# Routing in two phases: smaller pieces over more expert tiles, other steps for the first phase, and slots from one table

## The chip, the cores and the metric

The kernel runs on one core of a Trainium2 chip (trn2). The metric is the device time of one execution in microseconds (us), as the median of several runs. PE is TensorE (matmuls), DVE is VectorE, ACT is ScalarE, POOL is GpSimd, SP is SyncE, which only issues DMAs.

## The reference, cut to what matters

64 images are cut into 36 patches each, normalised and projected to 256 features; with one class token and 32 text tokens that is 69 tokens per image, 4416 tokens in all. Then one attention layer per image (16 heads of 16) and one mixture of experts with a residual each:

```python
h = concat([tokenizer(x), txt], axis=1)              # (64, 69, 256)
h = h + attention(layernorm(h))                      # per image
xn = layernorm(h).reshape(4416, 256)
logits = xn @ router                                 # (4416, 8)
top, idx = top_k(logits, 2); gate = softmax(top)
# each token goes to its 2 experts, sorted by expert:
y = (silu(x_sort @ w13[e][:, :512]) * (x_sort @ w13[e][:, 512:])) @ w2[e]
h = h + scatter_add(y * gate)
```

## The kernel before, in words

**Two stages with a seam.** The first stage is a pipeline by hand over steps `t`, one image per step (`step(t)` on each engine). Tables such as `PJ`, `QT`, `LG`, `ZM`, `BT` say in which step a tile of 128 tokens (35 of them) has its q, k projection, its logits, or its patch projection. In step t, PE multiplies the scores of image t, DVE takes their maximum (`nm_src`, L1090), PE multiplies the scores again transposed for image t-2 (L1622, L1626) once that maximum is there, and ACT takes their exponential. A step with a projection (in `PJ`; here 46, 48, 49, 51, 53, 55, 57, 59, 61) has six matmuls of 512 columns more on PE and two large operations more on DVE (`rot`, L1136, and `qk`, L1142). Every engine works through its list in order and waits on semaphores.

From `MERGE` (step 66) on, the second stage runs: 76 expert tiles `u` of 128 token slots, in `merged(...)`. For each, POOL gathers the rows of its tokens from HBM by the indices in `token_of` (L396), PE turns them (`turn_rows`, L560), ACT and DVE split them into two halves of 16 bits (`fx_hi` L455, `fx_lo` L484), PE multiplies gate and up (`up`, 12 matmuls of 512 columns, L520), ACT takes silu (L447), DVE multiplies (L477) and splits (L491), a DMA transposes, PE multiplies down (`down`), DVE weighs the result (L500) with the token's gate (L507, L512) and POOL adds it into `out` by an indirect DMA (L419). PE's `up(u+1)` needs `fx_lo` of tile u+1, which DVE makes right behind L477 of tile u. What is left of the first stage (`drain`: the last attention steps, logits of the last token tiles, up to `LAST_STEP`) lies between these pieces, as does `route(u)`, which comes last in each u on DVE.

**The routing** says which token goes to which slot of which tile. It is done in two phases: token tiles 0 to 19 (`AHEAD`) while attention runs, so that 33 tiles that are surely full can start at step 66; token tiles 20 to 34 during expert tiles, so that the other 43 tiles are known before tile 33. The pieces, all on DVE if nothing else is said: `choose` and `choose_second` (best and second best expert per token, L934 to L952), `open_gates` (exponential of the difference, on ACT) and `gates`, `count` (one-hot tables in 16 bits), `add_places` (on PE: running numbers of the tokens per expert, by matmuls with a triangle of ones, L1458 to L1469), `rank` (picks each token's number, splits it into lane and tile number), `bases_...` and `homes_...` (first tile of each expert, tile of each token), `mark_lanes` (14 tables of 640 columns: which lane, L1037), `mark_tiles` (which tile, L1042), `number` (on POOL: times the token's number, L750), `place` (on PE, L1479), `tokens_...`, `experts_of`, `behind`, and `weigh` (on POOL: gates per expert, stored to HBM by SP). Constants like `REV ... HOMES`, `LANES`, `IN_TILES`, `NUMBERED` give the step t of each piece of the first phase, the `U_...` the tile u of the second. In DVE's step the pieces stand at the end, in the order of `step(t)`; only the patch projection's `z` (L1240) comes behind them.

In phase 1 before, `choose` is at step 47, `choose_second` 49, `gates` 51, `count` 53, `rank` 54, `bases_ahead` 55, `homes_ahead` 56, the lanes at 57 to 60 (two each), the tile tables at 59 (3), 60 (3), 61 (2), the tokens at 62. In phase 2 `choose` is at u = 6, `choose_second` and `count` at 7, `add_places` on PE and `open_gates` on ACT at 8, `rank` and `gates` 9, `bases_later` 10, `homes_later` 11 with two lanes, two lanes each at 12 and 13, tile tables 13 to 19, `place` on PE 15 to 21, `tokens_later` 22, `experts_of` 23, `behind` 24.

## Time and profile before

| what | value |
|---|---|
| three runs | 777.3, 778.82, 774.69 us (median 777.3) |
| the profiled execution's own time | 773.16 us |
| its span, first to last instruction | 771.4 us |
| busy: PE, DVE, ACT, POOL | 687.5, 559.9, 403.0, 449.9 us |
| TensorE's clock, mean of the span | 0.954 of full |

Busy time is the sum of an engine's instruction times. A window's row gives, for a stretch of the span in us, its length and each engine's busy time with the number of instructions in brackets, then the granted clock of TensorE (1.00 is 2.4 GHz, 0.50 is 1.2 GHz) and the DMA share. A timeline row gives start, duration, engine, line, operation, output and inputs with their shapes, how many were merged, and in square brackets how long the engine stood idle before it and what released it.

### The profile page before, as it was taken

What the parts mean: (1) busy time and instruction counts of PE and PEld (TensorE: products, weight loads), DVE (VectorE), ACT (ScalarE), POOL (GpSimd) and SP (SyncE); (2) the same over time, 40 slices, a digit from 0 to 9 for tenths busy, and PEclk for the clock granted to TensorE, in tenths of its full rate; (3) what the DMA queues carried; (4) which work ended last, traced back from release to release, by engine and by line L of the source; (5) the groups of instructions that cost most, each with busy time, mean ns of one, the idle gap of its engine ahead of it and who ended that gap; (6) DMA issues with size and microseconds to landing.
All of it is one profiled execution on the core that took longest, in us unless ns stands there. A gap on an engine that the chain in (4) does not pass through costs nothing. (4 is left out here: it accounts for less than half of the span.)

```text
span 771.4 us, 27556 instructions
## 1 busy us (share of the span) xinstructions
PE 687.5 (89%) x9656; PEld 477.0 (62%) x9656; DVE 559.9 (73%) x1204; ACT 403.0 (52%) x884; POOL 449.9 (58%) x632
## 2 busy tenths in 40 slices
PE   6855998999999999987978898799999999999993
PEld 4633676767667777665656565466566666666662
DVE  6876888888887888889994567966755655655652
ACT  1233567677788787777655444333344444443440
POOL 7572255556566666546544375587566666665653
PEclk9987899999999999999885999999999999999998
DMA  8677566455555465545432485677677777777863
GB/s 289 225 211 250 151 208 219 139 151 170 177 155 171 136 180 151 157 128 148 112 110 61 100 132 103 95 125 118 112 131 128 127 134 129 127 134 133 123 127 60
DMA packets 145434, 112.53 MB, mean 146 GB/s; under 512 B 93544, under 2 KB 126072, under 8 KB 145239
## 3 DMA queue, kind: packets, MB, share of 16 engines
q1 hardware_dynamic: 129927, 86.75, 42.9%
q0 software_dynamic: 15376, 24.01, 18.1%
q8 instruction: 85, 1.39, 0.8%
q14 instruction: 46, 0.38, 0.2%
HBM read 58.95 MB, written 24.90 MB: 109 GB/s over the span
## 5 line engine op out<-in xcount | busy, mean ns | idle before, releaser
L419 POOL DMA_INDIRECT out<-qk,token_of x76 | 123.1, 1620 | 99.1 <-DVE small L507 75.4
L520 PE MATMUL quad<-w_hi,fx_hi 128*128 x304 | 116.1, 382 | 12.1 <-issue 9.9
L477 DVE SCALAR_TENSOR_TENSOR probs<-quad,up_scale,vb 128x512 f32<-128x512 f32 x76 | 57.0, 751 | 88.4 <-PE quad L520 86.1
L520 PE MATMUL quad<-w_lo,fx_hi 128*128 x304 | 115.9, 381 | 0.0
L520 PE MATMUL quad<-w_hi,fx_lo 128*128 x304 | 115.7, 381 | 0.0
L520 PE MATMUL bank<-w_hi,v 128*128 x608 | 111.9, 273 | 2.5 <-DMA v<-kO 2.5
L447 ACT ACTIVATE vb<-quad,unscale 128x512 f32<-128x512 f32 x76 | 52.2, 687 | 105.1 <-PE quad L520 105.1
L1090 DVE TENSOR_REDUCE nm_src<-quad 69x16 f32<-69x1104 f32 x64 | 82.8, 1294 | 24.5 <-PE quad L1558 24.2
L1341 ACT ACTIVATE probs<-quad 69x1104 f32<-69x1104 f32 x64 | 69.7, 1088 | 57.1 <-PE quad L1626 57.1
L396 POOL DMA_INDIRECT wc<-xn_rows,token_of x73 | 74.8, 1025 | 24.0 <-issue 20.2
L520 PE MATMUL bank<-w_lo,v 128*128 x304 | 82.9, 273 | 0.0
L729 POOL TENSOR_TENSOR rs<-ve,eps_pow 128x1 f32<-128x1 f32 (+1 forms) x106 | 63.0, 594 | 8.8
L728 POOL TENSOR_SCALAR ve<-mv 128x1 f32<-128x1 f32 (+1 forms) x106 | 28.0, 265 | 64.5 <-DVE mv L1153 33.9
L520 PEld LDWEIGHTS bank<-w_hi,v 128*128 128x128 f16 x608 | 59.5, 98 | 9.0 <-issue 2.9
L764 POOL TENSOR_TENSOR h<-hb,att 128x256 f32<-128x256 f32 (+1 forms) x35 | 35.1, 1004 | 51.1 <-issue 29.8
L455 ACT ACTIVATE fx_hi<-bank 128x256 f16<-128x256 f32 x76 | 29.2, 384 | 64.2 <-PE bank L560 64.2
L1622 PE MATMUL quad<-qT,kE 32*69 32x69 f32 x1024 | 46.3, 252 | 16.5 <-DVE nm_src L1090 16.2
L772 POOL TENSOR_TENSOR qk<-rot 128x256 f32<-128x256 f32 (+1 forms) x35 | 33.4, 956 | 46.0 <-DVE rot L1136 46.0
L520 PEld LDWEIGHTS quad<-w_hi,fx_hi 128*128 128x128 f16 x304 | 29.9, 98 | 46.5 <-issue 16.1
L1622 PEld LDWEIGHTS quad<-qT,kE 32*69 32x69 f32 x1024 | 29.5, 144 | 40.4 <-DVE nm_src L1090 30.0
L1626 PE MATMUL quad<-nm,sel 32*69 32x69 bf16 x1024 | 51.6, 197 | 0.0
L520 PEld LDWEIGHTS quad<-w_hi,fx_lo 128*128 128x128 f16 x304 | 29.9, 98 | 33.0 <-issue 0.8
(282 smaller groups left out, 1770.4 us busy)
## 6 DMA issues: line engine op xcount, KB each, us to landing
w_lo<-in_experts_w SPq DMA_DIRECT2D x24, 512.0 KB, 6.1
w_raw<-in_experts_w SPq DMA_DIRECT2D x48, 256.0 KB, 4.5
xt<-in_patches SPq DMA_DIRECT2D x18, 384.0 KB, 5.6
h<-h_rows SPq DMA_DIRECT2D x34, 128.0 KB, 5.4
hb<-h_rows SPq DMA_DIRECT2D x34, 128.0 KB, 4.8
out<-h SPq DMA_DIRECT2D x34, 128.0 KB, 4.3
xn_rows<-xn SPq DMA_DIRECT2D x34, 128.0 KB, 4.8
vb<-v SPq DMA_DIRECT2D x30, 138.0 KB
```

The source lines that it names most:

```text
L396: nc.gpsimd.indirect_dma_start(xg[n % DEPTH], None, reach(xn_rows, n), bass.IndirectOffsetOnAxis(token_of[:, n:n + 1], 0)).then_inc(gather ...
L419: nc.gpsimd.indirect_dma_start(reach(out, n), bass.IndirectOffsetOnAxis(token_of[:, n:n + 1], 0), y[q], None, compute_op=ALU.add).then_inc ...
L447: nc.scalar.activation(silu[q], quad[:, 2 * q, :], ACT.Silu, scale=unscale[:, 1:2]).then_inc(d["silu_ready"], 1)
L477: nc.vector.scalar_tensor_tensor(out=hid[q], in0=quad[:, 2 * q + 1, :], scalar=up_scale[:, :], in1=silu[q], op0=ALU.mult, op1=ALU.mult).th ...
L520: last = nc.tensor.matmul(dst, x[:, k, :], w[:, bass.ds(col + k * (2 * width if width == HIDDEN else width), width)], start=(k == 0 and m ...
L729: nc.gpsimd.tensor_tensor(rs, ve, eps_pow[0:rs.shape[0], :], ALU.pow).then_inc(signal, 1)
L764: nc.gpsimd.tensor_tensor(h2[g % 2][0:r, :], hb[g % 2][0:r, :], att[0:r, :], ALU.add).then_inc(s["h2_ready"], 1)
L772: nc.gpsimd.tensor_tensor(qk[0:r, 0:HEADS, :].rearrange("p n (two d) -> p n two d", two=2), halves[:, 0], halves[:, 1, :, ::-1, :], ALU.ad ...
L1090: nc.vector.tensor_reduce(nm_src[b % 2][:, :].rearrange("p (g j) -> p g j", g=4)[:, :, 0:4], quad[0:SEQ, :, 0:4 * SEQ].rearrange("p g (j k ...
L1341: nc.scalar.activation(probs[b % 2][0:SEQ, :, :], quad[0:SEQ, :, 0:4 * SEQ], ACT.Exp, scale=HEAD_DIM ** -0.5).then_inc(s["probs_ready"], 1)
L1622: nc.tensor.matmul(quad[0:SEQ, g, j * SEQ:(j + 1) * SEQ], (kE, kO)[odd][band, c, at:at + SEQ], qT[band, c, at:at + SEQ], start=True, stop= ...
L1626: to = nc.tensor.matmul(quad[0:SEQ, g, j * SEQ:(j + 1) * SEQ], sel[band, j, :], nm[b % 2][band, :], start=False, stop=True)
```

## The change

* **Slots from one table.** `rank`, `by_expert` and `homes_...` go. The table of running numbers (token tile by expert, in PSUM) is turned into slots by expert as a whole (`spread`: 3 operations of 160 columns in phase 1, 4 of 280 in phase 2), and `slots` picks each token's slot once and cuts it into lane (low 7 bits) and tile (the rest). `bases_...` now count slots, not tiles. In phase 2 table and slots cover all 35 token tiles, so `add_places(1)` multiplies all of them again.
* **Phase 1** has other steps: `choose` 45, `choose_second` 48, ACT's `open_gates` 49, `gates` 50, `count` 51, `add_places`, `bases_ahead` and `spread` 52 (`add_places` now early in PE's step, before the scores of image 50), POOL's constants 53 as before, `slots` and `weigh` 54, lanes 55, 56, 58, 60, tile tables 59 (2), 60 (2), 61 (4). PE's projections behind step 52 wait for `spread` (they waited for `rank` at 54).
* **Phase 2** starts two tiles later and takes 18 tiles: `choose` 8, `choose_second` 9, `count` 10, `gates` and PE's `add_places` 11, `bases_later` and `weigh` 12, `spread` 13, `slots` 14, one lane each at 15 to 20, tile tables 15 to 21, `place` 17 to 23, the edges 22, `experts_of` 23, `tokens_later` 24, `behind` 25.
* **The exponential of phase 2** goes from ACT to POOL, as e to the power of the gap (128x15), at u = 10.
* **Logits of the last tiles** are multiplied one tile later than their transpose, at the start of the next tile, where PE waited for ACT's copy inside the same tile; `LAST_STEP` is one more.
* `tokens_...`: the additions per run become one reduction.

The diff, cut to its core:

```diff
-LAST_STEP = BATCH + 8
+LAST_STEP = BATCH + 9
-OUTSIDE = 1000.0
+OUTSIDE = 1000.0 * P
...
+                LG[LAST_STEP - 1] = LG.pop(back[G - 1] + 3)
...
-                REV, FIRST_CHOICE, SECOND_CHOICE, GAPS, GATES, NUMBERS, RANK, SPLIT, HOMES = 40, 47, 49, 50, 51, 53, 54, 55, 56
-                LANES = {57 + k: range(2 * k, 2 * k + 2) for k in range(4)}
-                IN_TILES = {59: range(0, 3), 60: range(3, 6), 61: range(6, 8)}
-                NUMBERED = {60: range(0, 3), 61: range(3, 6), 62: range(6, 8)}
+                REV, FIRST_CHOICE, SECOND_CHOICE, GAPS, GATES, COUNT, RANK, NUMBERS, SLOTS = 40, 45, 48, 49, 50, 51, 52, 53, 54
+                LANES = {55: range(0, 2), 56: range(2, 4), 58: range(4, 6), 60: range(6, 8)}
+                IN_TILES = {59: range(0, 2), 60: range(2, 4), 61: range(4, 8)}
+                NUMBERED = {60: range(0, 2), 61: range(2, 4), 62: range(4, 8)}
                 TABLE, BEHIND = 62, 63
-                U_CHOICE, U_SECOND, U_RANK, U_GATES, U_SPLIT, U_HOMES = 6, 7, 8, 9, 10, 11
-                U_LANES = {11 + k: range(8 + 2 * k, 10 + 2 * k) for k in range(3)}
-                U_IN_TILES = {13 + k: range(2 * k, 2 * k + 2) for k in range(7)}
-                U_NUMBERED = {14 + k: range(2 * k, 2 * k + 2) for k in range(7)}
-                U_PLACED = {15 + k: range(2 * k, 2 * k + 2) for k in range(7)}
-                U_FOUND, U_EXPERTS, U_BEHIND = 22, 23, 24
+                U_CHOICE, U_SECOND, U_COUNT, U_GATES, U_BASES, U_SPREAD, U_SLOTS = 8, 9, 10, 11, 12, 13, 14
+                U_LANES = {15 + k: range(8 + k, 9 + k) for k in range(6)}
+                U_IN_TILES = {15 + k: range(2 * k, 2 * k + 2) for k in range(7)}
+                U_NUMBERED = {16 + k: range(2 * k, 2 * k + 2) for k in range(7)}
+                U_PLACED = {17 + k: range(2 * k, 2 * k + 2) for k in range(7)}
+                U_PASSED, U_EXPERTS, U_FOUND, U_BEHIND = 22, 23, 24, 25
...
+                        def open_gates():
+                            gap = choice[1]["gap"]
+                            pool.wait_ge(s["gap_ready"], 2)
+                            nc.gpsimd.tensor_tensor(gap, euler.broadcast_to([P, LATER]), gap, ALU.pow).then_inc(s["gates"], 1)
...
+                        def bases_later():
+                            dve.wait_ge(s["place_mm"], 2)
+                            then(nc.vector.scalar_tensor_tensor(out=count_i, in0=counts, scalar=float(P - 1), in1=full_ahead, op0=ALU.add, op1=ALU.subtract))
+                            then(nc.vector.tensor_scalar(count_i, count_i, -P, None, ALU.bitwise_and))
+                            then(nc.vector.tensor_copy(tiles_later, count_i))
+                            prefix_of(base_later, tiles_later, under[1])
+                            then(nc.vector.tensor_scalar(base_later, base_later, edges[:, EXPERTS - 1:EXPERTS], None, ALU.add))
+                            then(nc.vector.tensor_tensor(edges[:, EXPERTS:], base_later, tiles_later, ALU.add))
+                            then(nc.vector.memset(edges[:, 2 * EXPERTS - 1:], 2.0 * P * TILES_MOE))
+                            then(nc.vector.tensor_tensor(moved, base_later, edges[:, 0:EXPERTS], ALU.subtract))
+
+                        def spread(a):
+                            hi = PHASE[a][1]
+                            shape = [P, hi, EXPERTS]
+                            ranks = b4[:, 0:hi * EXPERTS].rearrange("p (g e) -> p g e", e=EXPERTS)
+                            then(nc.vector.tensor_tensor(table[a], ranks, full_ahead[:, None, :].broadcast_to(shape), ALU.is_ge))
+                            if a == 0:
+                                then(nc.vector.scalar_tensor_tensor(out=table[a], in0=table[a], scalar=OUTSIDE, in1=ranks, op0=ALU.mult, op1=ALU.add))
+                            else:
+                                then(nc.vector.tensor_tensor(table[a], table[a], moved[:, None, :].broadcast_to(shape), ALU.mult))
+                                then(nc.vector.tensor_tensor(table[a], table[a], ranks, ALU.add))
+                            nc.vector.tensor_tensor(table[a], table[a], base_ahead[:, None, :].broadcast_to(shape), ALU.add).then_inc(s["rank_ready"], 1)
+
+                        def slots(a):
+                            lo, hi = PHASE[a]
+                            shape = [P, TOP_K, hi, EXPERTS]
                             dve.wait_ge(s["rank_ready"], a + 1)
+                            then(nc.vector.tensor_tensor(own[a], pick[:, :, 0:hi, :], table[a][:, None, :, :].broadcast_to(shape), ALU.mult))
+                            with nc.allow_low_precision("whole numbers far below 2 ** 24"):
+                                then(nc.vector.tensor_reduce(slot[a], own[a], AX.X, ALU.add))
+                            then(nc.vector.tensor_scalar(lane_at[a], slot[a][:, :, lo:hi], P - 1, None, ALU.bitwise_and))
+                            then(nc.vector.tensor_scalar(tile_at[a], slot[a], -P, None, ALU.bitwise_and))
...
+                        def number_found(a, runs, width):
+                            for run in range(1, runs):
+                                then(nc.vector.tensor_scalar(b4[:, (runs + run - 1) * width:(runs + run) * width], b4[:, run * width:(run + 1) * width],
+                                                             0.5, float(run * RUN * P), ALU.is_ge, ALU.mult))
+                            then(nc.vector.tensor_reduce(found[a], b4[:, 0:(2 * runs - 1) * width].rearrange("p (r t) -> p t r", t=width), AX.X, ALU.add))
...
-                            nc.tensor.matmul(b4[:, lo * EXPERTS:hi * EXPERTS], prefix_h, both[:, lo:hi, :].rearrange("p g e -> p (g e)"),
+                            nc.tensor.matmul(b4[:, 0:hi * EXPERTS], prefix_h, both[:, 0:hi, :].rearrange("p g e -> p (g e)"),
...
+                            if MERGE < t <= LAST_STEP and t - 1 in LG:
+                                pe.wait_ge(s["xn2T_ready"], upto(LG, t - 1))
+                                logits_of(t - 1)
+                            if t < LAST_STEP and t in LG:
+                                pe.wait_ge(s["tokens_ready"], 1)
+                                pe.wait_ge(s["logits_saved"], upto(LG, t - 1))
                                 turn_normed(t)
-                        def after(u):
-                            t = MERGE + u
-                            if t < LAST_STEP and t in LG:
-                                pe.wait_ge(s["xn2T_ready"], upto(LG, t))
-                                logits_of(t)
```

## Rows read from the trace of the kernel before

**Rows 1.** Windows: attention step 45, 47-50, 51-54, 52 alone, 55-58, 59-60, 61-62.
```profile
303.41:309.48 6.07, 6.07 (x122) 4.97 (x121) 3.75 (x10) 4.43 (x14) 2.90 (x8) 1.00 0.76 226
...
314.67:337.98 23.31, 21.58 (x468) 16.09 (x466) 20.49 (x45) 16.98 (x43) 13.83 (x25) 0.93 0.43 130
337.98:359.51 21.53, 19.21 (x468) 13.98 (x468) 19.44 (x43) 17.39 (x44) 12.53 (x30) 1.00 0.48 134
343.13:347.55 4.42, 3.06 (x104) 2.33 (x103) 3.40 (x8) 4.22 (x13) 3.21 (x7) 1.00 0.31 82
359.51:382.21 22.70, 18.57 (x444) 14.50 (x444) 21.98 (x44) 15.03 (x38) 12.41 (x19) 0.85 0.51 130
382.21:394.47 12.26, 9.15 (x219) 7.07 (x218) 11.59 (x23) 7.36 (x18) 5.72 (x11) 0.84 0.40 119
394.47:407.56 13.09, 11.70 (x263) 8.70 (x264) 10.44 (x21) 7.32 (x17) 6.61 (x12) 0.76 0.37 104
```

**Rows 2.** What PE waited for from 300 to 425 us: total, times, longest.
```profile
PE quad L1622 <- DVE nm_src L1090: 9.8, 10, 2.7
```

**Rows 3.** Windows of expert tiles: u = 0-5, 6-14, 15-21, 22-23, one steady tile.
```profile
425.78:455.41 29.63, 27.25 (x198) 16.90 (x198) 17.09 (x44) 13.09 (x30) 15.71 (x20) 1.00 0.61 113
455.41:502.16 46.75, 39.15 (x254) 24.00 (x253) 38.77 (x109) 18.00 (x30) 27.23 (x22) 1.00 0.68 109
502.16:533.83 31.67, 31.42 (x254) 20.93 (x253) 20.27 (x52) 11.92 (x21) 27.15 (x29) 1.00 0.74 119
533.83:544.74 10.91, 9.90 (x66) 6.26 (x64) 9.59 (x28) 3.79 (x7) 6.32 (x6) 1.00 0.62 106
569.41:573.53 4.12, 4.12 (x28) 2.59 (x27) 2.46 (x6) 1.70 (x3) 2.59 (x3) 1.00 0.98 131
```

**Rows 4.** DVE's timeline: the first operation of a steady tile.
```profile
573.53 0.75 DVE L477 SCALAR_TENSOR_TENSOR probs<-quad,up_scale,vb 128x512 f32<-128x512 f32 x1 [1.25 <-PE quad L520]
```

**Rows 5.** DVE's timeline: routing operations of phase 1.
```profile
317.75 0.32 DVE L935 TENSOR_TENSOR w_lo<-logits,w_lo 128x160 f32<-128x160 f32 x1
...
375.47 2.08 DVE L1037 TENSOR_TENSOR xt<-gain,zout 128x640 f16<-128x640 f32 x2
...
399.47 1.93 DVE L1042 TENSOR_TENSOR wc<-gain,z 128x165 f16<-128x165 f32 x2
```

**Rows 6.** DVE's timeline: routing operations of phase 2.
```profile
479.10 0.17 DVE L1005 TENSOR_SCALAR shift<-shift 128x8 int32<-128x8 int32 x1
479.31 0.81 DVE L1006 CAST shift<-shift 128x8 f32<-128x8 int32 x1
...
487.54 1.56 DVE L1037 TENSOR_TENSOR rope_sb<-gain,zout 128x640 f16<-128x640 f32 x2
```

**Rows 7.** ACT's timeline at u = 8.
```profile
466.93 1.28 ACT L1287 ACT_TABLE_LOAD   x1
```

**Rows 8.** DVE's timeline behind that.
```profile
470.53 0.75 DVE L477 SCALAR_TENSOR_TENSOR probs<-quad,up_scale,vb 128x512 f32<-128x512 f32 x1 [2.17 <-ACT vb L447]
```

**Rows 9.** PE's timeline: logits at u = 0; first and last of `add_places(1)`.
```profile
428.22 0.61 PE L1517 MATMUL bank<-router_sb,xn2T 128*128 128x8 f32 x4 [1.27 <-ACT xn2T L1279]
...
465.64 0.23 PE L1458 MATMUL bank<-shift,bias 128*128 128x120 f16 x1
...
466.11 0.32 PE L1469 MATMUL bank<-shift,bias 128*128 128x8 f16 x7
```

**Rows 10.** POOL's groups by shape: the power, an addition, `number` in phases 2 and 1.
```profile
L729 POOL TENSOR_TENSOR rs<-ve,eps_pow 128x1 f32<-128x1 f32 x104 | 61.8, 594 | 8.7
...
L728 POOL TENSOR_SCALAR ve<-mv 128x1 f32<-128x1 f32 x104 | 27.2, 262 | 60.2 <-DVE mv L1153 29.6 <-DVE mv L1163 16.3 <-ACT zout L1398 4.6
...
L750 POOL TENSOR_TENSOR oT<-oT,shift 128x215 f16<-128x215 f16 x14 | 11.3, 1116 | 0.0
...
L750 POOL TENSOR_TENSOR wc<-wc,shift 128x165 f16<-128x165 f16 x4 | 1.8, 480 | 0.0
```

**Rows 11.** Window: from step 62 to the end of the first `up` matmuls.
```profile
405.00:424.70 19.70, 17.68 (x324) 12.99 (x324) 7.75 (x21) 10.62 (x22) 8.61 (x12) 0.50 0.20 60
```

More of the change, by code:

```diff
@@ L1012, in bases_later @@
-                            then(nc.vector.tensor_tensor(spent, base_later, full_ahead, ALU.subtract))
-                            then(nc.vector.scalar_tensor_tensor(out=moved, in0=spent, scalar=-OUTSIDE, in1=base_ahead, op0=ALU.add, op1=ALU.subtract))
-                        def homes_ahead():
-                            by_expert(limit, own[0], 0, AHEAD, full_ahead)
-                            then(nc.vector.tensor_tensor(beyond, part_f[0], limit, ALU.is_ge))
-                            by_expert(home, own[0], 0, AHEAD, base_ahead)
-                            then(nc.vector.tensor_tensor(home, home, part_f[0], ALU.add))
-                            then(nc.vector.scalar_tensor_tensor(out=tile_f[0], in0=beyond, scalar=OUTSIDE, in1=home, op0=ALU.mult, op1=ALU.add))
@@ L1215, in step @@
                                 count(0)
+                            if t == GATES:
+                                gates(0)
                             if t == RANK:
-                                dve.wait_ge(s["consts"], 6 + RUNS)
-                                rank(0)
-                            if t == SPLIT:
                                 bases_ahead()
-                            if t == HOMES:
-                                homes_ahead()
+                                spread(0)
+                            if t == SLOTS:
+                                dve.wait_ge(s["consts"], 5 + RUNS)
+                                slots(0)
                             for n in LANES.get(t, ()):
@@ L1257, in route @@
                             if u == U_GATES:
-                                rank(1)
                                 gates(1)
-                            if u == U_SPLIT:
+                            if u == U_BASES:
                                 bases_later()
-                            if u == U_HOMES:
-                                homes_later()
+                            if u == U_SPREAD:
+                                spread(1)
+                            if u == U_SLOTS:
+                                slots(1)
                             for n in U_LANES.get(u, ()):
@@ L1368, in step @@
                                      scale=unscale[0:r, 0:1])
[L1369 to L1375 removed]
+                            if t in LG and t < MERGE:
+                                save_logits(t)
                             if t + 1 in ZM and ZM[t + 1] < EARLIEST:
@@ L1672, in step @@
                                 to.then_inc(s["z_mm"], 1)
-                            if t == RANK:
-                                add_places(0)
                             if t == TABLE:
@@ L1719, in route @@
                                 place(n, in_tile_later[n], TILES_LATER, GROUPS, PLACED_AHEAD)
-                        merged(up, before, turn_rows, down, after, route)
+                        merged(up, before, turn_rows, down, route)
         front()
```

201 lines of the change are left out of this document (85 added, 116 removed).

## The prediction

> **What bounds the kernel now.** I read the page first (PE busy 89%, DVE 73%), then windows cut at the steps, since an average over both stages says little about a change at the seam, then DVE's, PE's, ACT's and POOL's timelines there.
>
> In attention steps 47 to 62 DVE is the bound: it works 20.49 of 23.31 us, 19.44 of 21.53, 21.98 of 22.70, 11.59 of 12.26 [rows 1]. Step 52, without routing, takes 4.42 us and DVE stands idle 1.0 in it; I take 4.42 as the floor of a step, set by PE and ACT. PE waits 9.8 us for DVE's maximum between 300 and 425 us [rows 2].
>
> In the expert stage PE is the bound: a steady tile takes 4.12 us with PE busy throughout [rows 3], and DVE stands idle 1.25 us of it [rows 4]. So a routing piece of up to 1.25 us on DVE is free; what exceeds it makes L477 late, hence `fx_lo` of the next tile, hence PE. Against 4.12 a tile, u = 0-5 lose 29.63 - 24.72 = 4.9 us, u = 6-14 lose 46.75 - 37.08 = 9.7, u = 15-21 lose 2.8, u = 22-23 lose 2.7 [rows 3]: 20.1 in all. The 2.8 is PE's own work (70 placing matmuls, 0.4 a tile) and stays.
>
> **A price list for DVE.** 160 columns take 0.32 us, 640 columns 0.78 (half of the pair's 1.56) [rows 5, 6]: about 0.17 us and 0.96 ns a column, plus 0.04 to the next one that depends on it; an operation of 8 columns 0.2. For shapes not in the trace (280, 560, 688 columns) this line gives 0.48, 0.75, 0.87. If reading PSUM or writing integers cost more, I allow a quarter on these, 1 us over all.
>
> **Phase 1, stretch by stretch** [rows 1].
> - Step 45: `choose` (six operations of 160, 2.1) comes in. DVE stood idle 6.07 - 3.75 = 2.3 there, but `z`, behind it, becomes later, and the next projection waits for `z`: +0.3.
> - 47-50: `choose` leaves, `choose_second` (1.8) moves from 49 to 48, `gates` (0.6) comes to 50. DVE's work falls by 1.5, but step 47 can't go below the floor and 48 is a projection step: -1.2.
> - 51-54: `gates` and `rank` (two of 320 columns, seven small: 2.3) leave; `bases_ahead` and `spread` (six small, three of 160: 2.4) and `slots` (1.5) come. That is 1.0 more, and step 52 had 1.0 idle: 0. `add_places` now runs on PE while it waits for DVE's maximum.
> - 55-58: `bases_ahead` (1.1) and `homes_ahead` (four of 320, three small: 2.8) leave, one pair of lanes more comes (1.6 to 2.1 [rows 5, 6]). Step 57 keeps no routing and stops at the floor: -1.9.
> - 59-60: one pair of lanes and two tile tables (0.3 each) leave: 2.4 of DVE, from 12.26 towards twice the floor, 8.84, but 0.5 us of the stretch is already PE's: -1.9.
> - 61-62: two tile tables more on DVE (0.6), and POOL numbers four tables in step 62 instead of two; PE's placing and DVE's tokens wait for them, 2 x 0.48 [rows 10]; the reduction in `tokens_ahead` gives 0.2 back: +1.3.
>
> Sum -3.4, with 0 (each gap handed on) and -6 as ends. SP's store of the gates moves up two steps and waits for POOL's `weigh` one step after it is issued; behind it on SP's queue lies the load of `vb` for an image three steps away, so I cost it at nothing. If POOL were later than three steps, PE would wait for `vb`.
>
> **Phase 2, tile by tile.** What exceeds 1.25 us:
> - u = 0-7: PE's wait of 1.27 for ACT's copy [rows 9] goes; behind it comes the wait for `fx_lo` of tile 1, and the logits' 0.6 lies in front of the next tile's rows: -0.5 of the 4.9.
> - 8 and 9: `choose`, `choose_second`, 1.95 and 1.93: +0.7 each.
> - 10: `count`, 0.8: nothing.
> - 11: `gates`, 0.6: nothing on DVE. But PE's `add_places(1)` takes 0.8 (465.64 to 466.43) [rows 9], hidden before because `fx_lo` was late anyway; now it is not, and 720 columns more at 2.4 GHz are 0.3: +1.1.
> - 12: `bases_later`, nine small, 1.8, and POOL's `weigh` beside them as before, where a copy of 8 columns took 0.81 instead of 0.17 [rows 6]: +1.2.
> - 13: `spread`, four of 280, 1.9: +0.7. 14: `slots`, two of 560 and two small, 2.0: +0.7.
> - 15 and 16: one lane and two tile tables, 1.5: +0.25 each. 17 to 20: the same beside PE's placing (0.4 a tile): nothing. 17 to 23: +2.8 for placing, as before.
> - 22: edges, two of 688, 1.74 against 1.25 + 0.4: +0.1. 23 to 25: 1.2, 1.4, 0.7: nothing.
>
> That is 8.5 where u = 6-23 lost 15.2, so -6.7, and with the first line -7.2. ACT's table load of 1.28 us [rows 7] (one into the exponential, one back), behind which L477 waited 2.17 us [rows 8], goes; it lies within the 9.7.
>
> **The power on POOL** is the unknown price. One column takes 0.594 us, an addition of one column 0.262 [rows 10]. For 15 columns the near end is 0.6 (all of it overhead), the far end 15 x 0.594 = 8.9; I take 0.26 + 15 x 0.33 = 5.2, as if only the overhead were shared. POOL reaches it about when the next tile begins; DVE asks for it 4.12 - 1.25 = 2.9 us later, and in that tile PE has 1.1 of `add_places` and DVE 0.65 free behind: 4.6 are free, 5.2 cost 0.6, 8.9 cost 4.3. With the near end as likely I enter +0.3. Behind it on POOL wait one gather, wanted two tiles later, and one scatter.
>
> **Sum:** -3.4 - 7.2 + 0.3 = -10.3. The profiled execution, 773.16 us, becomes 762.9; it lies 4.1 under the median of the runs shown, so 777.3 becomes **767.0**. With the ends of the terms (phase 1 from 0 to -6, phase 2 from -4 to -8.5) the forecast's own range is 763 to 772.
>
> **Rivals.**
> 1. *Phase 1 gives nothing.* The pieces at 48, 51, 55, 59 and 61 are still in steps with a projection, so the change does only half of what it says there, and from 61 on the bunched tables and four numberings could eat what 55 to 60 gain. For: the clock stood at 0.84 to 0.85 in 55-58 and 59-60 [rows 1], so that PE's floor there may lie above 4.42. Against: 2.4 us of DVE work truly go. 767.0 + 3.4 = 770.4.
> 2. *DVE and POOL collide.* A pair of tile tables took 1.93 us in step 61 [rows 5], against some 0.6 for two by the price list, with POOL at work beside it; the copy in rows 6 shows the same. In u = 16 to 20 a lane table now stands beside two numberings of 1.116 us each [rows 10]. If one operation per tile waits for one numbering, less the 0.2 still free, five tiles lose 0.9: 771.5. Against: in u = 15-21 tile tables ran beside numberings, and the stretch lost no more than PE's placing. The Trainium skill (SBUF — State Buffer, "Who interferes with whom") says that a DVE instruction with two SBUF inputs and a GpSimd instruction that reads SBUF exclude each other for a whole instruction; by that rule this rival is the forecast, and the change, which sets lanes beside numberings where they were apart, would come out at 771.5. The 0.81 us of rows 6 agree with the rule, the stretch u = 15-21 doesn't show it.
> 3. *The clock.* TensorE ran at 0.50 (1.2 GHz) from 405 to 424.7 us with PE busy 17.68 of 19.70 [rows 11], behind steps in which PE had waited for DVE, and at 0.76 to 0.85 in 55-62 [rows 1]. If fewer waits keep it at 2.4 GHz, I estimate that a quarter of that stretch goes, 5 us: 762.0. Against: PE's longest waits come in 61 and 62, which the change fills more.
> 4. *Slower.* POOL's power is far dearer than its one-column form. DVE waits for it in u = 11, everything behind on POOL too. It decides from 4.6 + 10.6 + 3.9 = 19 us on (781.2), that is 1.27 us a column, twice what a whole instruction of one column takes. I price it at 25 us: 787.
>
> **How the numbers follow.** A measurement of this kernel tells about 0.5% (3.9 us) from no change. Forecast 0.56, rival 1 0.11, rival 2 0.11, rival 3 0.10, rival 4 0.05, and 0.07 that terms I don't see bring it back to 774 to 779. Below 773.4 lie the forecast, rivals 1 to 3 but for 0.03 of theirs: faster 0.85; same 0.09; slower 0.06. The range reaches from rival 3 to just beyond rival 2: 761 to 773; left out are 0.12 above and some 0.05 below.
>
> **What would show it.** Right: steps 57 and 59 near 4.5 to 5 us, 48 and 55 longer; no table load behind the first expert tile; u = 8 to 14 each between 4.1 and 5.4; u = 22 to 25 at PE's pace; PE's `add_places` with no wait behind it. Wrong: L1037 of 1 us and more in u = 16 to 20 (rival 2), a DVE wait before `gates` in u = 11 (rival 4), steps 45 to 62 as long as before (rival 1), the clock at 1.00 from 405 us on (rival 3).

## The result and the profile after

The changed kernel took 765.9 us (median of four runs, 765.4 to 767.76) beside 777.4 of the kernel before (774.69 to 778.82): a ratio of 0.9887 with a 95% interval of 0.9846 to 0.9928. A repeat of six runs, at the end of the study, gave 0.9809 (0.9765 to 0.9852). Both intervals lie below 1: it is faster, by some 1 to 2%. The forecast was 767.0.

The profiled execution took 765.4 us, span 763.6. First the windows of the changed kernel, on the borders of [rows 1] and [rows 3]: step 45, 47-50, 51-54, 52, 53, 55-58, 57, 59-60, 61-62, from step 63 to the first expert tile, then u = 0-5, 6-14, 15-21 and 22-23. Columns as there: length, busy PE, PEld, DVE, ACT, POOL, granted clock, DMA share, GB/s.

```profile
305.11:311.17 6.06, 6.06 (x122) 4.96 (x121) 5.61 (x15) 4.41 (x14) 2.95 (x8) 1.00 0.72 212
316.37:339.11 22.74, 21.56 (x468) 16.20 (x466) 19.09 (x41) 17.02 (x44) 13.64 (x25) 0.92 0.45 133
339.11:362.03 22.92, 18.90 (x460) 13.78 (x461) 19.75 (x45) 16.25 (x41) 12.75 (x30) 0.93 0.46 128
344.94:350.61 5.67, 3.20 (x114) 2.46 (x112) 5.33 (x17) 5.54 (x15) 4.03 (x10) 1.00 0.36 99
350.61:357.15 6.54, 6.10 (x114) 3.92 (x115) 4.13 (x8) 1.80 (x6) 2.46 (x5) 0.74 0.23 61
362.03:383.71 21.68, 18.04 (x450) 13.79 (x449) 19.63 (x34) 15.36 (x41) 13.23 (x20) 0.92 0.53 142
372.89:378.82 5.93, 5.88 (x118) 4.08 (x116) 4.19 (x7) 3.08 (x7) 3.25 (x6) 0.82 0.40 115
383.71:393.36 9.65, 8.61 (x227) 6.43 (x226) 9.55 (x18) 7.80 (x18) 4.94 (x8) 1.00 0.45 134
393.36:406.29 12.93, 10.08 (x258) 7.69 (x257) 10.29 (x22) 7.04 (x16) 8.42 (x15) 0.85 0.37 107
406.29:424.20 17.91, 16.14 (x277) 11.25 (x279) 6.82 (x17) 9.28 (x17) 7.36 (x9) 0.54 0.17 48
424.20:452.34 28.14, 25.93 (x191) 16.44 (x192) 17.20 (x44) 12.49 (x28) 15.06 (x19) 1.00 0.57 116
452.34:494.24 41.90, 40.24 (x267) 25.33 (x268) 32.15 (x91) 15.68 (x30) 30.54 (x23) 1.00 0.77 125
494.24:526.31 32.07, 31.07 (x228) 19.80 (x226) 27.78 (x63) 11.52 (x20) 26.97 (x26) 1.00 0.82 118
526.31:535.81 9.50, 9.29 (x75) 6.03 (x74) 7.81 (x19) 3.40 (x6) 8.42 (x9) 1.00 0.79 88
```

Read against [rows 3], the gain is in the expert stage: u = 0-23 took 29.63 + 46.75 + 31.67 + 10.91 = 118.96 us and now take 28.14 + 41.90 + 32.07 + 9.50 = 111.61, 7.35 less. PE, idle for 7.6 us of u = 6-14 before, is idle for 1.7. Steps 45 to 62 took 407.56 - 303.41 = 104.15 us and now take 406.29 - 305.11 = 101.18, 2.97 less. The bill of the two profiled executions: step 45 begins 1.70 us later (305.11 against 303.41), though nothing in front of it was changed; -2.97; -0.31 from step 63 to the first tile (a stretch that takes 17.89 to 19.14 us over the runs below that add nothing to it); -7.35; +0.85 for one gather that came late in tile 27; +0.27 for the rest. The sum is -7.8, as the spans say (771.4 and 763.6). The stretches that the change touches give -10.6; the forecast was -10.3.

What PE waited for from 300 to 425 us, beside [rows 2]:

```profile
PE quad L1631 <- DVE nm_src L1091: 5.5, 7, 1.4
...
PE bank L1438 <- DVE w_lo L1019: 1.9, 1, 1.9
```

The wait for DVE's maximum fell from 9.8 us to 5.5. The second line is new: the projection of step 53 waits for the last operation of `spread` (L1019). The last one to read the table of running numbers in PSUM is the operation before it (L1015); L1019 reads SBUF alone. DVE's timeline there shows how it comes back: `rot` waits 1.22 us for that projection, and the next maximum 1.13.

```profile
349.66 0.32 DVE L1013 TENSOR_TENSOR w_lo<-bank,shift 128x160 f32<-128x160 f32 x1
350.02 0.32 DVE L1015 SCALAR_TENSOR_TENSOR w_lo<-w_lo,bank 128x160 f32<-128x160 f32 x1
350.37 0.32 DVE L1019 TENSOR_TENSOR w_lo<-w_lo,shift 128x160 f32<-128x160 f32 x1
...
353.78 1.22 DVE L1137 TENSOR_TENSOR rot<-bank,rope_sb 128x1024 f32<-128x1024 f32 x1 [1.22 <-PE bank L1438]
...
357.15 1.30 DVE L1091 TENSOR_REDUCE nm_src<-quad 69x16 f32<-69x1104 f32 x1 [1.13 <-PE quad L1565]
```

The unknown price, POOL's power of 15 columns, and DVE's wait for it:

```profile
474.73 3.35 POOL L754 TENSOR_TENSOR w_raw<-small,w_raw 128x15 f32<-128x15 f32 x1
```

```profile
478.11 0.18 DVE L978 TENSOR_SCALAR w_raw<-w_raw 128x15 f32<-128x15 f32 x1 [0.35 <-POOL w_raw L754]
```

### The profile page after: what moved, and what is told of

The parts are those of the page before. It is cut to its first block and busy times, and to the rows that moved or that the text cites. A ratio compares the mean times of both kernels' runs of the same rounds, so it can differ in the third digit from the quotient of the medians.

```text
span 763.6 us, 27530 instructions
## 1 busy us (share of the span) xinstructions
PE 688.8 (90%) x9656; PEld 477.0 (62%) x9656; DVE 555.8 (73%) x1182; ACT 398.6 (52%) x881; POOL 457.5 (60%) x634
## 3 DMA queue, kind: packets, MB, share of 16 engines
q8 instruction: 85, 1.39, 0.8%
## 5 line engine op out<-in xcount | busy, mean ns | idle before, releaser
L481 DVE SCALAR_TENSOR_TENSOR probs<-quad,up_scale,vb 128x512 f32<-128x512 f32 x76 | 57.0, 751 | 79.9 <-PE quad L524 77.8
L1438 PE MATMUL bank<-wqkv_hi,fx_hi 128*128 128x512 f16 (+2 forms) x140 | 49.8, 356 | 2.8 <-DVE w_lo L1019 1.9
```

What stands on the lines that cost most here:

```text
L481: nc.vector.scalar_tensor_tensor(out=hid[q], in0=quad[:, 2 * q + 1, :], scalar=up_scale[:, :], in1=silu[q], op0=ALU.mult, op1=ALU.mult).th ...
L1438: to = nc.tensor.matmul(dst, x[g % 2][:, k, 0:r], w[:, k, cols], start=(k == 0 and m == 0), stop=(k == KD - 1 and m == 2))
```

## The experiments

Every run is the changed kernel with the edit shown. Whole runs of one kernel differ by up to 2% (e2: 762.01 to 777.13 us; the repeat: 758.89 to 770.0), more than most edits here can move, and so do the starts of step 45 (298.8 to 308.1 us over the profiles). The single steps, measured between the starts of DVE's maxima in the timeline, repeat to some 0.02 us in most cases where the clock is the same (the largest difference is 0.16: step 58 takes 4.89 us, in e5b 5.05). So I read stretches. This table is made from those starts; "low" is the time at 1.2 GHz in steps 45 to 62, twice (1 - granted clock) times the length, summed over the steps.

| run | 47+48 | 52-54 | 57 | 45-62 | low |
|---|---|---|---|---|---|
| before | 10.94 | 16.38 | 6.11 | 104.15 | 20.5 |
| changed kernel | 11.92 | 17.09 | 5.93 | 101.18 | 14.3 |
| the same, repeated | 11.10 | 19.62 | 4.50 | 101.89 | 20.5 |
| e2, these steps unchanged | 11.10 | 19.63 | 4.51 | 101.55 | 19.9 |
| e3, unchanged | 11.80 | 16.97 | 5.88 | 100.91 | 14.2 |
| e5a, unchanged | 11.10 | 19.63 | 4.60 | 102.17 | 21.0 |
| e5b, unchanged | 11.92 | 17.08 | 5.93 | 101.34 | 14.4 |
| e1 old steps | 9.87 | 15.97 | 7.00 | 102.53 | 14.6 |
| e4 early release | 11.97 | 17.75 | 4.61 | 101.03 | 17.3 |
| e7 tables early | 11.10 | 19.62 | 5.58 | 101.34 | 20.2 |
| e8 second choice in 47 | 9.58 | 16.81 | 7.35 | 100.83 | 16.0 |
| e10 busy in 53 | 11.11 | 15.46 | 7.31 | 101.13 | 17.1 |
| e11 busy to the drain | 11.10 | 16.66 | 6.80 | 100.86 | 16.7 |
| e12 busy in all places | 10.85 | 16.51 | 6.26 | 104.52 | 14.3 |

**The old steps, with the new table (e1).**

```diff
-REV, FIRST_CHOICE, SECOND_CHOICE, GAPS, GATES, COUNT, RANK, NUMBERS, SLOTS = 40, 45, 48, 49, 50, 51, 52, 53, 54
-LANES = {55: range(0, 2), 56: range(2, 4), 58: range(4, 6), 60: range(6, 8)}
-IN_TILES = {59: range(0, 2), 60: range(2, 4), 61: range(4, 8)}
-NUMBERED = {60: range(0, 2), 61: range(2, 4), 62: range(4, 8)}
+REV, FIRST_CHOICE, SECOND_CHOICE, GAPS, GATES, COUNT, RANK, NUMBERS, SLOTS = 40, 47, 49, 50, 51, 53, 54, 53, 55
+LANES = {57 + k: range(2 * k, 2 * k + 2) for k in range(4)}
+IN_TILES = {59: range(0, 3), 60: range(3, 6), 61: range(6, 8)}
+NUMBERED = {60: range(0, 3), 61: range(3, 6), 62: range(6, 8)}
```

> The changed kernel with the first half's routing put back on the steps it had before: choices in 47 and 49, gates in 51, counts in 53, bases and the table in 54, slots in 55, lanes by pairs in 57 to 60, tile tables 3, 3, 2 in 59 to 61. It keeps the one small table (less DVE work) and everything in the expert stage. From the start of step 45 to the start of step 63 the kernel before took 104.15 us, the changed one 101.18. Theory (work and place both count: some 2.4 us of DVE work less, and pieces that leave steps with a projection): 102.4, within 0.6, that is half of the gain without the new steps. Rival (only the new steps count): 104.0. Second rival (only the work counts, where it stands does not matter): 101.2. The expert stage, from the first tile's down-projection mark (339.4 us to the end), should stay within 0.5 us in every case.

Steps 45 to 62 took 102.53 us: by its number the middle case. Read so, some 1.6 of the profile's 2.97 us come with the smaller work alone, and the new steps add 1.4, or 1.0 against the mean of the six profiles in which these steps are the changed kernel's (101.5; they run from 100.91 to 102.17). This division isn't shown: it compares single profiles, and 102.53 lies only 0.36 above the longest of the six. The three of them with e1's low time (14.2 to 14.4) took 100.91 to 101.34, which speaks for a gain from the new steps. Ratio 0.9873 (0.9764 to 0.9981), too wide to tell it from the changed kernel; u = 8 to 14 took what they took there.

**The later routing packed (e2).**

```diff
-U_CHOICE, U_SECOND, U_COUNT, U_GATES, U_BASES, U_SPREAD, U_SLOTS = 8, 9, 10, 11, 12, 13, 14
-U_LANES = {15 + k: range(8 + k, 9 + k) for k in range(6)}
+U_CHOICE, U_SECOND, U_COUNT, U_GATES, U_BASES, U_SPREAD, U_SLOTS = 8, 9, 9, 10, 11, 12, 12
+U_LANES = {13 + k: range(8 + 2 * k, 10 + 2 * k) for k in range(3)}
```

> The changed kernel with the later routing packed: second choice and count together in expert tile 9, gates in 10, bases in 11, table and slots together in 12, lanes by pairs in 13 to 15; the tile tables stay in 15 to 21. The same instructions, five fewer tiles to hold them. The changed kernel loses 8.4 us against 4.12 us a tile over tiles 8 to 23 and 27. Theory (each tile has 1.25 us of DVE free, and only what exceeds it costs): tile 9 holds 1.93 + 0.8 (excess 1.5 instead of 0.7 and 0), tile 12 holds 1.9 + 2.0 (2.65 instead of 0.7 + 0.7), tiles 13 to 15 hold two lanes each, 1.6 (0.35 each), and 15 to 20 lose their lane: in all 2.0 us more for the expert stage. Rival (the total of DVE's work sets the time, not its shares): no change, within 0.4. Second rival (lanes beside POOL's numberings cost more than the packing): 1 us less.

Windows of u = 8-14 and 15-26 of this run:

```profile
456.10:490.87 34.77, 31.09 (x204) 19.07 (x203) 30.06 (x82) 11.91 (x21) 23.79 (x19) 1.00 0.78 115
490.87:544.71 53.84, 52.95 (x381) 33.71 (x378) 39.43 (x104) 20.44 (x36) 43.03 (x39) 1.00 0.80 117
```

And of the changed kernel:

```profile
461.48:494.24 32.76, 31.10 (x209) 19.60 (x208) 26.85 (x79) 12.28 (x22) 25.53 (x20) 1.00 0.71 123
494.24:548.13 53.89, 52.63 (x376) 33.21 (x373) 44.59 (x107) 20.03 (x35) 42.95 (x39) 1.00 0.82 115
```

PE has the same work in u = 8-14 (31.09 and 31.10 us busy) and needs 34.77 - 32.76 = 2.01 us longer for it; u = 15-26 took 0.05 less: 1.96 in all, where 2.0 was expected. Tile 9 took 5.42 us, 1.30 above 4.12 (1.5 by the theory), tile 12 took 6.70, 2.58 above (2.65 by the theory). DVE's free 1.25 us a tile are a budget that a tile can't lend to the next one; this is what the smaller pieces buy.

**The exponential back on ACT (e3).**

```diff
-                            if u == U_COUNT:
-                                open_gates()
...
+                            if u == U_COUNT:
+                                gap = choice[1]["gap"]
+                                act.wait_ge(s["gap_ready"], 2)
+                                nc.scalar.activation(gap, gap, ACT.Exp).then_inc(s["gates"], 1)
```

> The changed kernel with the later exponential back on ACT (at the end of its work in expert tile 10, waiting for the gaps) instead of the power on POOL; DVE's and PE's work is the same. ACT loads a table twice at 1.28 us. Theory (the copies of ACT into SBUF feed PE's next tile, and two loads in a row of two tiles make them late): the exponential's load stands beside tile 10 and the one back in front of tile 11's copies, 1.1 us longer for the expert stage (339.4 to 340.5), all of it in tiles 10 to 12. Rival (the loads fall in ACT's idle time, some 1.5 us of a tile): within 0.3 of 339.4.

ACT's timeline has the two loads, and DVE's shows that `hid` (L481) waits for the copy behind the second:

```profile
470.01 1.28 ACT L1426 ACT_TABLE_LOAD   x1
...
471.54 1.28 ACT L451 ACT_TABLE_LOAD   x1
```

```profile
473.61 0.75 DVE L481 SCALAR_TENSOR_TENSOR probs<-quad,up_scale,vb 128x512 f32<-128x512 f32 x1 [1.33 <-ACT vb L451]
```

u = 8-14 took 33.44 us, 0.68 more, but not by the loads. Tile 10, where both stand, rose by 0.94, and tile 11 fell by 0.93, to 4.09, because PE's `add_places(1)` was hidden again behind an `fx_lo` that was late anyway: two delays that cover each other aren't added. So the loads cost nothing, as the rival says, if for another reason. The 0.68 come from tiles 12 (+0.92) and 13 (-0.26). POOL, here without the power, came to `weigh` in tile 12, beside `bases_later`, and three small operations of DVE took 0.78, 0.30 and 0.43 us instead of 0.23, 0.17 and 0.17. The first of them and `weigh` in e3, then in the changed kernel, where `weigh` began behind that tile (tile 13 begins at 484.63):

```profile
481.60 0.78 DVE L1002 TENSOR_SCALAR shift<-shift 128x8 f32<-128x8 f32 x1
...
482.30 0.97 POOL L746 TENSOR_TENSOR zout<-pick,w_raw 128x120 f32<-128x120 f32 x1
```

```profile
483.82 0.23 DVE L1004 TENSOR_SCALAR shift<-shift 128x8 f32<-128x8 f32 x1
...
485.25 0.96 POOL L746 TENSOR_TENSOR zout<-pick,w_raw 128x120 f32<-128x120 f32 x1
```

In e2 the two met as well, in tile 11, which took 5.42 us, 1.30 above 4.12. The whole runs (763.14 us median, 760.32 to 764.9) don't resolve it.

**PE released earlier in step 52 (e4).**

```diff
+nc.vector.tensor_copy(ranks_own, b4[:, 0:AHEAD * EXPERTS]).then_inc(s["ranks_read"], 1)
+nc.vector.tensor_copy(count_i, counts).then_inc(s["ranks_read"], 1)
...
+ranks = (ranks_own if a == 0 else b4[:, 0:hi * EXPERTS]).rearrange("p (g e) -> p g e", e=EXPERTS)
...
-                                    pe.wait_ge(s["rank_ready"], 1)
+                                    pe.wait_ge(s["ranks_read"], 2)
```

> The changed kernel with one copy more on DVE in step 52: the 160 ranks and the counts are copied out of PSUM first, and PE's projection in step 53 waits for these copies alone instead of the finished table (1.9 us of waiting in the changed kernel, and DVE idle 1.22 us behind it). Theory (that wait is on the path): step 53 from 6.54 to about 4.9 us, step 52 or the next 0.4 longer for the copy, 1.2 less over steps 52 to 54. Rival (PE would wait in step 53 for DVE's maximum or its clock instead): steps 52 to 54 stay at 17.1 us, within 0.4.

Steps 52 to 54 took 17.75 us, 0.66 more. The wait moved: the projection ran in step 52 at full clock, PE then waited 2.46 us for DVE's maximum, and the clock fell to 0.77 in step 53 and 0.61 in 54. That is the rival's account, though not its number, since the edit has a cost of its own: step 52 took 6.74 us instead of 5.67. PE's timeline, DVE's, then POOL's:

```profile
353.21 0.36 PE L1636 MATMUL quad<-qT,kE 32*69 32x69 f32 x8 [2.46 <-DVE nm_src L1096]
```

```profile
350.04 0.74 DVE L1018 TENSOR_TENSOR w_lo<-w_lo,shift 128x160 f32<-128x160 f32 x1
350.82 0.77 DVE L1020 SCALAR_TENSOR_TENSOR w_lo<-w_lo 128x160 f32<-128x160 f32 x1
```

```profile
349.87 0.74 POOL L816 TENSOR_TENSOR zout<-zout,gain 128x256 f32<-128x256 f32 x1
350.68 0.72 POOL L818 TENSOR_TENSOR zout<-zout,shift 128x256 f32<-128x256 f32 x1
```

The first two operations of `spread`, 0.32 us each while one input lay in PSUM, took 0.74 and 0.77 with both in SBUF, ending up to 0.2 us behind POOL's two operations. In the changed kernel L1015, with an input in PSUM, ran in 0.32 us inside POOL's L816 (349.73 to 350.45). The Trainium skill (SBUF — State Buffer, "Who interferes with whom") says that a DVE instruction with two SBUF inputs contends with a GpSimd instruction that reads SBUF, and one with at most one SBUF input does not, outside DVE's 2-port modes; both traces agree. Whether the wait itself cost anything stayed open here.

**Lane and tile tables apart, two ways (e5a, e5b).**

```diff
-U_IN_TILES = {15 + k: range(2 * k, 2 * k + 2) for k in range(7)}
+U_IN_TILES = {15 + k: range(k, k + 1) for k in range(6)} | {21: range(6, 8), 22: range(8, 11), 23: range(11, 14)}
```

> The changed kernel with one tile table, one numbering and one placing in each of expert tiles 15 to 20 and up (the rest in bunches: two tables in 21, three in 22 and 23), the closing pieces two tiles later (24 to 27). The same instructions. Above 4.12 us a tile the changed kernel loses 5.2 us over tiles 15 to 25. Theory (a DVE table and a lane table are slowed by POOL's numberings beside them, and one numbering a tile is hidden): 15 to 20 near 4.3 us instead of 4.1 to 4.8, the bunched ones 0.3 worse each, in all 1.2 us less over tiles 15 to 27. Rival (PE's placing and the total of DVE's work set it): within 0.4 of the changed kernel over tiles 15 to 27.

```diff
-U_LANES = {15 + k: range(8 + k, 9 + k) for k in range(6)}
-U_IN_TILES = {15 + k: range(2 * k, 2 * k + 2) for k in range(7)}
+U_LANES = {15 + k: range(8 + 2 * k, 10 + 2 * k) for k in range(3)}
+U_IN_TILES = {18 + k: range(2 * k, 2 * k + 2) for k in range(7)}
```

> The changed kernel with the six later lane tables by pairs in expert tiles 15 to 17, and the tile tables after them, in 18 to 24 (numbered one tile later, placed two later), so that no lane table stands beside a numbering on POOL. Theory of a collision (a DVE operation with both inputs in SBUF is held up by POOL's, the tile tables at 0.8 us instead of 0.38): the tile tables behind lanes come back towards 0.4 us, and tiles 15 to 27 together lose 0.8 us less than in the changed kernel (5.2). Second theory (from the run with lanes by pairs in 13 to 15, where tiles 18 to 23 together were 0.35 us shorter): 0.3 less. Rival (no collision to be had back): no change, within 0.2.

Numbering, placing and the closing pieces moved along, the last of them into u = 27. A pair of tile tables in the changed kernel, first in a tile without numberings on POOL, then in two with them:

```profile
497.75 0.67 DVE L1043 TENSOR_TENSOR oT<-gain,z 128x215 f16<-128x215 f32 x2
...
501.84 1.09 DVE L1043 TENSOR_TENSOR oT<-gain,z 128x215 f16<-128x215 f32 x2
...
506.39 1.16 DVE L1043 TENSOR_TENSOR oT<-gain,z 128x215 f16<-128x215 f32 x2
```

With the lanes first (all seven pairs are like the first row's), and with one table a tile (six like the second):

```profile
512.68 0.67 DVE L1043 TENSOR_TENSOR oT<-gain,z 128x215 f16<-128x215 f32 x2
```

```profile
497.33 0.38 DVE L1043 TENSOR_TENSOR oT<-gain,z 128x215 f16<-128x215 f32 x1
```

Now u = 15-27 as a whole, in the changed kernel's repeat (in its first profile a gather came late in tile 27), with one table a tile, then with the lanes first:

```profile
498.23:556.23 58.00, 56.74 (x404) 36.08 (x402) 46.97 (x113) 21.73 (x38) 45.05 (x41) 1.00 0.75 120
493.82:551.85 58.03, 56.72 (x404) 35.83 (x402) 45.93 (x112) 21.73 (x38) 45.70 (x41) 1.00 0.81 118
493.09:551.62 58.53, 57.00 (x410) 36.52 (x408) 46.16 (x113) 22.11 (x39) 43.84 (x41) 1.00 0.75 120
```

Five pairs of the changed kernel are 0.4 to 0.5 us longer, in u = 16 to 20, where they stand behind a lane table in tiles with numberings on POOL. With the lanes first all five come back, with one table a tile all but one place (three tables in tile 22 took 1.38 us, three in tile 23 0.96). Which of POOL's instructions holds DVE up isn't shown: the first numbering's record begins as the slow table ends. DVE's busy time falls by 1.0 and 0.8 us. The stretch stays at 58.03 us with one table a tile, and with the lanes first it is 0.5 longer, in tile 27 (4.71 us), where two closing pieces now stand together. So both theories of a collision that costs time fall. PE is busy for all but 1.3 to 1.5 us of the stretch in the three layouts: PE's own work, the placing in it, sets the rest, wherever DVE's tables stand.

**Tile tables earlier in phase 1 (e7).**

```diff
-IN_TILES = {59: range(0, 2), 60: range(2, 4), 61: range(4, 8)}
-NUMBERED = {60: range(0, 2), 61: range(2, 4), 62: range(4, 8)}
+IN_TILES = {57: range(0, 4), 60: range(4, 6), 61: range(6, 8)}
+NUMBERED = {58: range(0, 4), 61: range(4, 6), 62: range(6, 8)}
```

> The changed kernel with the first half's tile tables earlier: four in step 57 (where DVE stood idle 1.7 us), two each in 60 and 61; POOL numbers four in 58 and two each in 61 and 62. The same instructions. The changed kernel takes 5.93 us in step 57 (4.5 where TensorE is granted its full clock, as in two of the runs before this), 5.11 in 59, 5.99 in 61, 6.94 in 62. Theory (DVE bounds 59 and 61, and POOL's four numberings bound 62): 59 and 61 fall to about 4.8 and 5.3, 62 to 6.0, while 57 stays: 1.9 us less from the start of step 45 to that of step 63 (101.2; the three runs with these steps unchanged gave 100.9 to 101.6). Rival (TensorE's clock, which falls to 1.2 GHz after steps in which it had little to do, takes it back): between 100.6 and 101.6.

Steps 59 and 61 fell to 4.47 and 5.53 us, and 62 stayed at 6.98 with its clock at 0.53. But step 57 took 5.58 with DVE busy for 5.51, where at the same full clock it takes 4.50 without tables. DVE's idle time in 57 had been there only because PE ran at half speed. In all 101.34: the rival's number, but not by its reason. The clock stood at 1.00 in 57; DVE's work there cost 1.1 us, about what 58, 59 and 61 gave back.

**The second choice in step 47 (e8).**

```diff
-... GATES, COUNT, RANK, NUMBERS, SLOTS = 40, 45, 48, 49, 50, 51, 52, 53, 54
+... GATES, COUNT, RANK, NUMBERS, SLOTS = 40, 45, 47, 49, 50, 51, 52, 53, 54
```

> The changed kernel with one number changed: the first half's second choice (1.8 us on DVE) in step 47, which has no projection and where DVE stood idle 1.3 us, instead of step 48, which has one. In the changed kernel steps 47 and 48 take 4.16 + 7.76 us. Theory (DVE bounds step 48, and PE's idle time in step 47 is what lets its clock fall in step 48): step 47 rises to 4.7, step 48 falls to 5.0, as in the run with the old steps, in all 2.2 us less. Rival (PE's projection at 1.2 GHz sets step 48 whatever DVE does): 48 falls to 6.1 only, in all 1.1 us less. Second rival (only the total of DVE's work counts): no change.

Windows of steps 47-48 and of 57:

```profile
313.33:322.91 9.58, 8.50 (x227) 6.39 (x225) 9.27 (x21) 7.93 (x21) 7.60 (x12) 1.00 0.38 117
367.92:375.27 7.35, 7.30 (x119) 4.88 (x117) 4.19 (x7) 3.08 (x7) 3.25 (x6) 0.65 0.55 155
```

Steps 47 and 48 took what the theory said, 9.58 us instead of 11.92 (11.10 in the profiles whose clock stayed up in step 48 without this edit). That PE's idle time in 47 brings the fall in 48 isn't shown: the clock stayed up there with the second choice in 48 (repeat, e2, e5a, e7), and fell to 0.79 with it in 47 (e12). The whole stretch, 100.83 us, is 0.35 below the changed kernel's profile and 0.08 below the shortest of the six: step 57 ran at clock 0.65 and took 7.35, and steps 49 and 50 took 0.7 more.

**PE kept busy (e10, e11, e12).** Matmuls whose results nothing reads, in a PSUM bank that is free there:

```diff
+def keep_busy(t):
+    if t in BUSY:
...
+        for _ in range(BUSY[t]):
+            nc.tensor.matmul(b6[:, 384:512], wqkv_hi[:, 0, 0:P], wqkv_hi[:, 1, 0:P], start=True, stop=True)
```

> The changed kernel with 28 matmuls of 128 columns, whose results nothing reads, on PE at the place where it waits 1.9 us for DVE's table ahead of the projection of step 53. TensorE's granted clock fell behind that wait in every run so far: steps 53 and 54 took 6.54 + 4.88 us (five runs, clock 0.74 in 53) or 8.46 + 5.49 (three runs, 0.50 and 0.6). Theory (PE standing idle in step 52 is what lets the clock fall, and the fall costs, not the wait): the clock stays at 1.00 in 53 and 54, the two take 5.5 + 4.9, and 45 to 63 is 1 us shorter than the shortest so far (100.9) unless the fall comes in a later step. Rival (the clock falls by itself at its times, or because of what PE did in earlier steps): 53 and 54 as in one of the two patterns, and the added matmuls cost nothing or 0.5 us.

> The same, and 16 such matmuls each ahead of the transposed scores of steps 63, 64 and 65, where the changed kernel's clock stood at 0.50 to 0.54 from step 63 to the first expert tile (17.9 us, PE busy in 16.1 of them). Theory (it is what PE does, small tiles and waits, that holds the clock at 1.2 GHz there, not what it did before): the clock comes up within these steps, the stretch falls from 17.9 to 14 or 15 us in spite of the added work (48 matmuls at 0.06 us, 3 us). Rival (the clock stays down whatever PE does): the stretch rises by twice the added work, to 22 us or more.

PE's timeline and the windows of steps 53, 57 and 59, with 28 such matmuls ahead of step 53's projection:

```profile
350.54 1.73 PE L1554 MATMUL bank<-wqkv_hi 128*128 128x128 f16 x28
352.58 0.38 PE L1438 MATMUL bank<-wqkv_hi,fx_hi 128*128 128x512 f16 x1 [0.31 <-DVE w_lo L1019]
```

```profile
352.13:357.06 4.93, 4.62 (x117) 3.32 (x115) 4.11 (x8) 1.81 (x6) 2.19 (x4) 1.00 0.21 53
372.77:380.08 7.31, 7.26 (x118) 4.84 (x116) 4.20 (x7) 3.08 (x7) 3.26 (x6) 0.64 0.49 142
384.98:391.04 6.06, 6.01 (x113) 3.48 (x111) 5.15 (x9) 3.28 (x7) 3.26 (x6) 0.73 0.34 105
```

Step 53, 6.54 us in the changed kernel and 8.47 in its repeat, took 4.93 at clock 1.00 (0.38 us a matmul instead of 0.63), though its projection began as late as ever, 0.45 us into the step (0.44). So the wait was nearly free; the half clock behind it was what cost. But the clock then fell in 57 and 59, which took 2.3 us more than in the changed kernel, and the stretch stayed at 101.13.

In e11 the same 28 matmuls didn't hold the clock. They ran into the fall, at nearly twice the time, and step 53 took 6.11 us at clock 0.84:

```profile
351.00 3.11 PE L1554 MATMUL bank<-wqkv_hi 128*128 128x128 f16 x28
```

In e11's drain the clock rose to 0.80, and the added work ate it: 18.38 us, where the runs without it took 17.89 to 19.14. Neither the 14 to 15 us of the theory nor the rival's 22 came.

> The changed kernel with the second choice in step 47, and PE kept busy (matmuls of 128 columns whose results nothing reads) in the places where it waited and where the clock fell afterwards: 28 ahead of the projection of step 53, 14 and 10 at the start of steps 55 and 57, 8 and 10 ahead of the transposed scores of 56 and 62. With the shortest duration that any run gave for each step, all of them at clock 1.00, steps 45 to 62 add up to 96.9 us. Theory (each fall follows PE standing idle in the step before, and a fall that is prevented in one place comes in the next place where PE stands idle): with these places filled, the clock stays at 1.00 up to step 61 and 45 to 63 takes 97 to 98 us, 3 us less than any run so far. Rival (the falls come about equally often whatever is filled): 100.5 to 101.5, as in all the runs of this study with the changed kernel's steps.

The same `keep_busy` in five places, with the second choice in step 47. Step 53 took 4.93 us again, at clock 1.00. Windows of 55-57 and of 45-62:

```profile
358.55:379.66 21.11, 18.81 (x359) 13.56 (x358) 15.05 (x26) 10.91 (x24) 10.63 (x14) 0.76 0.47 121
302.58:407.10 104.52, 93.20 (x2162) 70.87 (x2161) 89.15 (x182) 71.89 (x176) 58.29 (x106) 0.93 0.47 135
```

97 to 98 us were expected, 104.52 came: the clock fell in 55-57 all the same, and the added matmuls ran at 1.2 GHz there (93.20 us of PE; 87.96 to 90.54 in the six profiles with these steps unchanged). The low time, 14.3 us, is that of the changed kernel's profile without them. Median 767.33 us, ratio 0.9873 (0.9829 to 0.9916).

> The changed kernel itself, once more, to set the run above against and to narrow the interval of the result. By the runs so far: steps 45 to 63 in 100.9 to 102.2 us, the first 30 expert tiles 136.3 us plus single late gathers of up to 0.9 us, in all a ratio of about 0.987 to the kernel before; had the profiled execution's 10.6 us between the two kernels' changed stretches been chance, it would be nearer to 1.

The changed kernel again: median 765.01, ratio 0.9809 (0.9765 to 0.9852), steps 45-62 in 101.89, the first 30 tiles in 136.29 (143.63 before). The gain is no chance of one profile of the changed kernel; of the kernel before there is one profile. No version tried can be told from it as faster.

## Why the prediction was right

- **Phase 2** carried it: -7.35 us over u = 0-23 where -6.9 was forecast (-7.2, and 0.3 for the power). That the two are so near is in part luck, since two terms were off and cancel: u = 0-5 alone gave -1.49 (-0.5 for u = 0-7), and u = 6-23 gave -5.86 (-6.7). Tiles 6 and 7, put at nothing, lose 0.42 and 0.48.
- **The rule** held tile by tile: excess 0.55 and 0.54 us in u = 8, 9 (0.7 each forecast), none in 10, 0.90 in 11 (1.1), 0.73 and 0.64 in 13, 14 (0.7 each), and e2 shows the budget of 1.25 us directly. That `add_places(1)` would be uncovered in 11 was right: in e3, where `fx_lo` is late, tile 11 takes 4.09 us instead of 5.02.
- **u = 12** (1.2 forecast, 0.59 measured): the term priced POOL's `weigh` beside `bases_later`, but POOL came to `weigh` one tile later, at 485.25 us, in u = 13. The price itself was about right: where the two met, the excess was 1.30 (e2) and 1.51 (e3). Some 0.26 of u = 13's 0.73 came with `weigh` (e3, without it there: 4.59 us).
- **u = 15-23** was undersized: 2.8 us of placing and some 0.6 beside it were forecast, 4.5 measured. PE is busy 3.3 us beyond nine steady tiles (40.36 against 37.08) and idle for 1.2. The two edits of DVE's tables don't move the idle time; what causes it stays open.
- **The power** took 3.35 us, between the ends 0.6 and 8.9 and under my 5.2; DVE waited 0.35 us for it, within the 4.6 free. Rival 4 needed 19.
- **Phase 1** gave -2.97 in the profile (-3.4 forecast), about -2.6 by the mean of the unchanged runs. The size was right, its parts were not. "51-54: 0" is the step that failed: +1.39. The half clock behind the wait for `spread` wasn't in the sum; with the clock up in step 53 (e10) the four steps took 21.29 us, against 21.53 before, which is the 0 of the forecast. "61-62: +1.3" came out at -0.16: step 62 takes 6.98 us with two numberings (e7) and 6.99 with four (e2, e10) at about the same clock. 55-58 gave -1.02, not -1.9: step 57 lost its routing but not its length, 5.93 us, with PE busy for 5.88 at clock 0.82. Step 45 gave 0 (+0.3), 47-50 -0.57 (-1.2), 59-60 -2.61 (-1.9). In the profiles of the other kind, described at the end, 51-54 come to +3.9 and 55-58 to -2.4: only the sum is steady.
- **Rival 1** was half right about the mechanism (in e8 and e10 a step gained and the clock fell in another), wrong about the sum. **Rival 2**'s collision took place, in tile tables at 1.09 to 1.16 us a pair instead of 0.67, and cost nothing, since PE set those tiles; the lane tables that it named kept to 0.82. The Trainium skill's rule, as cited there, says who blocks whom, not what waits for it; "by that rule 771.5" was the error of adding it to the path. And the 0.81 us of rows 6, said to agree with the rule, are a cast with one input, which a rule on two inputs doesn't cover. **Rival 3**: the clock from step 63 to the first tile was 0.54, as before (0.53), so it didn't come.
- The base: the sum was made on a profiled execution 4.1 us under the median, and the medians differ by 11.5 us where the profiles differ by 7.8. The 1.70 us by which the profile after was late at step 45 are part of that; no instruction there was changed. That 767.0 lies within 1.1 us of the median is therefore luck in part; the forecast of the changed stretches, -10.3 against -10.6, is the better test.

## What to carry to other kernels

A bound engine with a steady period gives its helpers a budget per period; work cut to that budget is free, and two pieces in one period cost all that exceeds it, whatever stands empty beside them. Two engines blocking each other cost nothing where a third one sets the period (the tile tables, u = 16-20), and all of it where the blocked one does (tile 12 of e3, 0.92 us), so look at who ends last before paying to separate them. Where TensorE's clock moves, an idle gap seen in one profile may exist only because PE ran at half speed there: look at the same steps in a second profile before filling it.
